# Two-layer graph network: the packed adjacency turned by DMA as 16-bit numbers in place of TensorE transposes

## What is computed

```
deg = clip(adj.sum(1), 1); dis = deg ** -0.5
diffusion = (dis[:,None] * adj * dis[None,:]) @ x - x
sim  = cosine similarity of all pairs of rows of x
attn = softmax(beta * sim * adj, axis=1)
x1 = layernorm(x + diffusion + sigmoid(alpha) * (attn @ x - x))
out = layernorm(x1 + relu(adj @ (x1 @ weights)))
```

## Time and profile before

| | us |
|---|---|
| median of 3 runs | 677.5 (676.59 to 679.42) |
| the profiled execution's own time | 677.66 |
| span of the profiled execution, first to last instruction | 675.8 |
| PE busy | 652.8 |
| DVE busy | 534.2 |
| ACT busy | 414.1 |
| POOL busy | 244.9 |

### The profile page before, as it was taken

How to read it: one execution, slowest core, us unless ns; L and a number is a source line. 1 busy time by engine, 2 the same in 40 slices (tenths; PEclk the granted TensorE clock), 3 DMA queues, 4 the chain that set the end, 5 groups by cost and what they waited for, 6 DMA issues and landing times.

```text
span 675.8 us, 16373 instructions
## 1 busy us (share of the span) xinstructions
PE 652.8 (97%) x5143; PEld 470.1 (70%) x5143; DVE 534.2 (79%) x1598; ACT 414.1 (61%) x775; POOL 244.9 (36%) x229
## 2 busy tenths in 40 slices
PE   6779999999999999999999999899999999999996
PEld 6447777777777777777777777788888864444455
DVE  4879999999999999999999999877777762334442
ACT  5989899898998999988999988511111110000000
POOL 2899446446455465454465467300000000000000
PEclk8999999999999999999999999999999999999999
DMA  6589999999999999999999994300000000000000
GB/s 252 185 220 249 242 261 244 253 255 243 260 263 242 254 253 249 250 266 232 262 260 249 249 248 94 67 1 1 0 0 0 0 0 1 17 16 16 16 31 32
DMA packets 154539, 105.33 MB, mean 156 GB/s; under 512 B 135696, under 2 KB 136208, under 8 KB 154512
## 3 DMA queue, kind: packets, MB, share of 16 engines
q1 hardware_dynamic: 154080, 104.94, 61.0%
q10 hardware_dynamic: 432, 0.07, 0.1%
HBM read 69.34 MB, written 2.10 MB: 106 GB/s over the span
## 4 chain that ended last, share of the span: by engine, by line
PE 85%; DVE 4%; DMA 3%; POOL 3%; ACT 2%; SPq 1%; issue 1%; DVEq 0%; ACTq 0%; POOLq 0%
PE ps_s L974 21%; PE ps_s L1135 17%; PE ps_e L1107 14%; PE ps_e L1006 8%; PE ps_e L985 7%; PE ps_acc L1006 7%; PE ps_e L1009 4%; PE ps_acc L1009 3%; DMA eTx<-e_parts 2%; DVE e_parts L710 1%; DMA col<-in_L_gnn_beta 1%; PE ps_e L1022 1%; DVE scores L689 1%; PE ps_at L958 1%; SPq L242 1%; POOL x_parts L339 1%
## 5 line engine op out<-in xcount | busy, mean ns | idle before, releaser
L974 PE MATMUL ps_s<-xn_parts,xn_signed 128*128 128x512 f16 x756 | 203.7, 379 | 5.1 <-DVE cmax L689 5.1
L689 DVE CUSTOM_DVE_ANT_1 scores<-ps_s,adj_bytes 128x512 f32<-128x512 f32 x252 | 171.6, 683 | 17.1 <-PE ps_s L974 10.3
L500 ACT ACTIVATE scores<-scores,col 128x1024 f32<-128x1024 f32 x128 | 157.4, 1232 | 4.3 <-DVE col L700 4.1
L324 POOL TENSOR_SCALAR e_parts<-scores 128x1024 f16<-128x1024 f32 x64 | 84.0, 1313 | 158.2 <-ACT scores L500 93.0
L446 ACT ACTIVATE adj_bytes<-land 128x1024 uint8<-128x1024 f32 x128 | 133.5, 1047 | 1.8 <-POOL packed L316 1.8
L974 PEld LDWEIGHTS ps_s<-xn_parts,xn_signed 128*128 128x128 f16 x756 | 69.5, 98 | 41.3 <-DVE cmax L689 5.1
L1107 PE MATMUL ps_e<-y_parts,stage 128*128 128x256 f16 x896 | 98.0, 273 | 0.0
L710 DVE SCALAR_TENSOR_TENSOR e_parts<-scores,e_parts 128x1024 f16<-128x1024 f32 x64 | 97.0, 1516 | 0.9 <-POOL e_parts L324 0.9
L507 ACT ACTIVATE eT_parts<-ps_e 128x512 f16<-128x512 f32 x128 | 75.8, 592 | 32.0 <-PE ps_e L985 31.2
L1107 PEld LDWEIGHTS ps_e<-y_parts,stage 128*128 128x128 fp8e4 x896 | 87.7, 98 | 10.1
L704 DVE SCALAR_TENSOR_TENSOR eT_parts<-ps_e,eT_parts 128x512 f16<-128x512 f32 x128 | 87.5, 684 | 1.5 <-ACT eT_parts L507 1.5
(11 more groups left out here) (131 smaller groups left out, 1015.0 us busy)
## 6 DMA issues: line engine op xcount, KB each, us to landing
land<-in_adj SPq DMA_DIRECT2D x128, 512.0 KB, 4.7
x_keep<-in_x SPq DMA_DIRECT2D x4, 512.0 KB, 8.4
out<-u SPq DMA_DIRECT2D x7, 256.0 KB, 2.0
eTx<-e_parts SPq DMA_TRANSPOSE x64, 4.6
out<-u SPq DMA_DIRECT2D x2, 128.0 KB, 1.7
eT_parts<-in_L_gnn_weights ACTq DMA_DIRECT2D x1, 64.0 KB, 8.6
scores<-in_L_gnn_weights SPq DMA_DIRECT2D x1, 64.0 KB, 2.8
col<-in_L_gnn_alpha ACTq DMA_DIRECT2D x1, 0.5 KB, 5.6
```

The lines of the kernel that those rows point to most:

```text
L324: nc.gpsimd.tensor_scalar(e_parts[:, n, 0, :], scores[:, q, (n + 2) * CH:(n + 3) * CH], E_SCALE, 1.0, ALU.mult, ALU.mult).wait_op(sign_don ...
L500: nc.scalar.activation(piece, piece, ACT.Exp, bias=neg_max[q], scale=abs_beta, accum_out=csum[:, q, i:i + 1]).then_inc(exp_done, 1)
L689: nc.vector.tensor_tensor_reduce(scores[:, q, o:o + BANK].rearrange("p (k q) -> p k q", k=K), score_bank(h, r == 0 if start else False).re ...
L974: ins = nc.tensor.matmul(score_bank(h, start), xn_signed[:, q, part, :], xn_parts[:, other, o:o + BANK], start=(part == 0 and other == 0), ...
```

## The change

K becomes 2: a node's number is b*256 + 2*p + k, with 16 blocks b of 256 nodes. Two neighbouring bytes, a 16-bit number, now belong to one position of two blocks.

- A byte of the packed row holds two row blocks: the even row of a pair is cast to 128, 64, 32, 16, the odd one to 8, 4, 2, 1. `pack` of the even row is three additions as before; `pack` of the odd row adds its four pieces to the same word, so it is four.
- `turn_adj` leaves PE. Once in two rows the SP queue issues one DMA transpose of 128 partitions x 512 16-bit numbers (128 KB), 16 in all, directly into packT. In the loop it stands behind pieces 2 and 3 of a row and ahead of turn n = 0 of an odd row; the last one is behind the last turn.
- `store_adj` and its semaphore are gone, so DVE has one copy less a row. packT is half as large.
- `stage_block` reads the word of the pair and shifts left or, for the top bit, right. The number of instructions and their shapes stay.
- Order inside each bank of 512 columns: SLOT = (0, 2, 1, 3) names which block of x stands in which quarter. Mask, transposes, `attend` and `sign_block` use it; `sign_block` and `pack` on POOL are written out for four rows at a time.
- Moving and stationary fp8 reads have a step of 2 bytes and the mask's byte read too, in place of 4. x is loaded and the output stored in runs of 1 KB in place of 2 KB.

```diff
-K = 4
-BYTE_ONE = 64
+K = 2
+BYTE_TOP = (128, 8)
+BYTE_F8_BITS = 0x40404040
...
-        packT = sb("packT", [P, R, CH // K], U32)
+        packT = sb("packT", [P, R // 2 * W], U32)
...
-            sp.dma_start(x_b[:, 0:2, :], x_v[:, 0:2, :]).then_inc(x_loaded[0], 16)
-            for q in range(1, C):
-                sp.dma_start(x_b[:, 2 * q:2 * q + 2, :], x_v[:, 2 * q:2 * q + 2, :]).then_inc(x_loaded[q], 16)
+            for q in range(C):
+                sp.dma_start(x_b[:, 4 * q:4 * q + 4, :], x_v[:, 4 * q:4 * q + 4, :]).then_inc(x_loaded[q], 16)
...
+            def turn_adj(m, q):
+
+                sp.wait_ge(packed_done, 2 * m + 2)
+                sp.dma_start_transpose(packT[:, bass.ds(m * W, W)].bitcast(U16).rearrange("p (a i) -> p a i", i=P),
+                                       packed_half[q]).wait_op(x_loaded[0], 16, "sem-ge").then_inc(adj_turned, 16)
+
...
+            turn_adj(0, 0)
+            with sp.Fori(1, Q) as b:
+                for k in range(G):
+                    r, q = b * G + (k - 3), (k + 1) % 2
                     for i in range(C):
...
                         if i == 1:
                             turn_ex(r, q, 1)
+                    if k == 1:
+                        turn_adj(b * 2 + (-1), 1)
+                    if k == 3:
+                        turn_adj(b * 2, 0)
                     turn_ex(r + 1, 1 - q, 0)
             for r in (R - 3, R - 2, R - 1):
                 turn_ex(r, r % 2, 1)
                 if r < R - 1:
                     turn_ex(r + 1, (r + 1) % 2, 0)
+            turn_adj(R // 2 - 1, 1)
...
-            def pack(r, q, first=False):
+            def pack(r, q, m, s, first=False):
 
 
                 pool.wait_ge(cast_done, r * C + C)
...
+                if q == 0:
+                    if not first:
+                        pool.wait_ge(adj_turned, m * 16 - 16)
+                    nc.gpsimd.tensor_tensor(packed[:, s, :], words[q][:, 0, :], words[q][:, 1, :],
+                                            ALU.add).then_inc(pack_step, 1)
...
+                else:
+                    pool.wait_ge(packed_done, r)
+                    for i in range(C - 1):
+                        nc.gpsimd.tensor_tensor(packed[:, s, :], packed[:, s, :], words[q][:, i, :],
+                                                ALU.add).then_inc(pack_step, 1)
+                        pool.wait_ge(pack_step, m * 5 + (3 + i))
+                nc.gpsimd.tensor_tensor(packed[:, s, :], packed[:, s, :], words[q][:, 3, :],
                                         ALU.add).then_inc(packed_done, 1)
...
-            def store_adj(r):
-
-                dve.wait_ge(adj_turned, r + 1)
-                nc.vector.tensor_copy(packT[:, r, :], ps_at[:, 0:CH // K].bitcast(U32)).then_inc(adj_stored, 1)
-
...
+                    up = 6 - ((3 if n % 2 else 7) - i)
+                    nc.vector.tensor_scalar(stages[to][:, bass.ds(n, 1), i * W:(i + 1) * W],
+                                            packT[:, bass.ds(r * P + (-P if n % 2 else 0), W)].unsqueeze(1), abs(up),
+                                            BYTE_F8_BITS, ALU.logical_shift_left if up >= 0 else ALU.logical_shift_right,
                                             ALU.bitwise_and).then_inc(staged, 1)
...
-                    if h == 6:
-                        store_adj(r)
...
-                    if h == 1:
-                        turn_adj(r, q, start)
```

More of the change, by code:

```diff
@@ L202, in two_layer_gnn @@
         x_v = x.rearrange("(b p k) d -> p b (k d)", p=P, k=K)
-        out_v = out.rearrange("(b p k) d -> b p (k d)", p=P, k=K)
-        adj_v = adj.rearrange("(b p k) j -> b k p j", p=P, k=K)
+        out_v = out.rearrange("(g b p k) d -> g p b (k d)", b=G // K, p=P, k=K)
+        adj_v = adj.rearrange("(g b p k) j -> g b k p j", b=G // K, p=P, k=K)
         u_b = u[:, :, :].rearrange("p (b k) d -> p b (k d)", k=K)
@@ L218, in two_layer_gnn @@
         words = [adj_bytes[:, q, :].bitcast(U32).rearrange("p (i w) -> p i w", i=C) for q in range(2)]
-        packed_f = [packed[:, q, :].bitcast(F32) for q in range(2)]
+        packed_half = [packed[:, m, :].bitcast(U16) for m in range(2)]
         stages = [land[:, :, :].bitcast(U32), stage[:, :, :]]
@@ L247, in _ @@
                 land_piece(0, 0, i)
-            for k in range(1, K):
+            for k in range(1, G):
                 for i in range(C):
@@ L251, in _ @@
                     land_piece(0, k, i)
-                    if k == K - 1 and i == 1:
+                    if k == G - 1 and i == 1:
                         turn_ex(0, 0, 1)
-                if k == K - 2:
+                if k == G - 2:
                     turn_ex(0, 0, 0)
-                if k == K - 1:
+                if k == G - 1:
                     turn_ex(1, 1, 0)
-            with sp.Fori(1, B) as b:
-                for k in range(K):
-                    r, q = b * K + (k - 3), (k + 1) % 2
+            turn_adj(0, 0)
+            with sp.Fori(1, Q) as b:
+                for k in range(G):
+                    r, q = b * G + (k - 3), (k + 1) % 2
                     for i in range(C):
-                        sp.wait_ge(cast_done, b * (K * C) + ((k - 1) * C + i + 1))
+                        sp.wait_ge(cast_done, b * (G * C) + ((k - 1) * C + i + 1))
                         land_piece(b, k, i)
@@ L273, in _ @@
             sp.dma_start(wts, weights).then_inc(w_loaded, 16)
[L274 to L280, removed]
+            with sp.Fori(0, Q - 1) as g:
+                sp.wait_ge(out_done, g * G + G)
+                sp.dma_start(out_v[g], u_b[:, bass.ds(g * 2, 2), :]).then_inc(out_stored, 16)
+            for b in range(2):
+                sp.wait_ge(out_done, R - 2 + 2 * b)
+                sp.dma_start(out_v[Q - 1, :, b, :], u_b[:, B - 2 + b, :]).then_inc(out_stored, 16)
+            sp.wait_ge(out_stored, 16 * (Q + 1))
         @block.gpsimd
@@ L348, in _ @@
             for i in range(C):
-                nc.gpsimd.memset(deg_unit[:, i:i + 1], float(1 << i) / BYTE_ONE).then_inc(deg_step, 1)
+                for q in range(2):
+                    nc.gpsimd.memset(deg_unit[:, i, q:q + 1], 1.0 / (BYTE_TOP[q] >> i)).then_inc(deg_step, 1)
             unit_rows(1)
@@ L359, in _ @@
             x_split(1)
-            pack(0, 0, first=True)
+            pack(0, 0, 0, 0, first=True)
             ex_high(0, 0, 0, first=True)
             ex_high(0, 0, 1, first=True)
-            sign_block(2, 0)
+            sign_block(2, 0, 2)
             x_split(2)
@@ L366, in _ @@
             ex_high(1, 1, 0)
-            pack(1, 1, first=True)
+            pack(1, 1, 0, 0)
             ex_high(1, 1, 1)
-            sign_block(3, 1)
+            sign_block(3, 1, 3)
             pool.wait_ge(sigma_done, 1)
@@ L403, in _ @@
             ex_high(R - 2, 0, 1)
-            pack(R - 1, 1)
+            pack(R - 1, 1, R // 2 - 1, 1)
             pool.wait_ge(dis_done, 1)
@@ L590, in _ @@
             keep_z(0, G)
-            for j in range(1, B - 1):
+            for j in range(1, Q - 1):
                 keep_z(j, G)
                 roots(j - 1, G)
[L594 to L598, removed]
+            keep_z(Q - 1, 2)
+            roots(Q - 2, G)
+            keep_z(Q, 2)
+            roots(Q - 1, 2)
+            roots(Q, 2)
         @block.vector
@@ L916, in _ @@
                 stage_block(G + n, n)
-            for j in range(1, B):
+            for j in range(1, Q):
                 relu_add(j - 1, (j - 1) * G, G)
-                if j < B - 1:
+                if j < Q - 1:
                     dve.wait_ge(z_done, j)
@@ L948, in turn_rows @@
                 ins.then_inc(xnt_turned, 1)
[L950 to L960, removed]
             def cosines(r, q, h, start=False):
@@ L1004, in attend @@
                     else:
-                        hi, lo = (eTx[:, q, b // 2 - 2, a * TC + t % TC, :] for a in range(2))
+                        hi, lo = (eTx[:, q, b // 2 - 2, a * TC + slot, :] for a in range(2))
                     nc.tensor.matmul(attn_ps[q][:, 0:2 * D], hi, x_parts[:, t, :],
```

107 lines of the change are left out of this document (52 added, 55 removed).

## The result

| | before | changed |
|---|---|---|
| median | 677.24 us (4 runs) | 665.62 us (4 runs, 664.87 to 666.40) |
| ratio to before | | 0.9828, 95% interval 0.9814 to 0.9841 |
| profiled execution, time and span | 677.66, 675.8 | 666.40, 664.5 |

The account below looks back on a forecast made before the run. PE was taken to bound the row phase without slack, with the SP queue 0.6 us a pair behind and taking over after the change. 677.7 + 6.0 - 0.7 - 0.5 = 682.5 us, range 667 to 693.

Parts of the forecast that it names:

- PE's two transposes: Row phase on PE: removing them frees 0.22 us a row, 0.44 in a pair, 7.0 us over 32 rows.
- DVE's copy and POOL's additional addition: Copy hidden in the row phase, 0.7 us saved behind the last rows; addition hidden, 0 with bounds -0.8 and +0.8.
- the 0.7 + 0.5 of the sum: Savings of 0.7 us for two DVE copies behind the last rows and 0.5 for PE's slots in rows 0, 1, 30, 31.
- The 16 DMA turns: SP queue in the row phase: 1.03 us more in a pair, lengthening pairs by 0.43, +6.0 us in all.
- a turn isn't put out before what stands ahead of it on the queue has nearly drained: SP queue: turns end some 4.6 to 5.0 us after the landings were issued, read as waiting for the drain.
- four halves of 6.1 us are the least: SP queue's least time for a pair of rows, taken as 24.4 us beside 25.0 measured.
- a slack of 0.6 us: SP queue's spare time in a pair of rows, seen as idle DMA engines from 252.50 to 253.00 us.
- Its upper bound: New turns on the SP queue: 1.32 us to put out whatever the size, no overlap, 26.35 a pair, +19 us.
- 0.33 if it goes with size: Time to put out a new turn on the SP queue, scaled from 1.32 us for 2048 numbers.
- The reads with a step of 2: Second layer's fp8 matmuls: 0 taken, bounds -4.6 and 0 us, as jumps between row blocks could explain the times too.
- x in runs of 1 KB: Loading x at the very start: 0 taken, bounds -0.5 and +1.5 us.
- Rival B with the reads: Turn fits into idle half microsecond before odd row's T0 turn, PE stays bound: 670 us, 665.7 if reads count; chance 0.33.

Follow-up runs that it names:

- pe_back: Changed kernel with two dummy 128 x 128 f32 transposes a row put back on PE, without DVE's copy: 671.37 us.
- before_flat4: Kernel before, second layer reading each 512 columns out of one row block at a step of 4 bytes, no jumps: 677.49 us.
- after_step4: Changed kernel, second layer reading the staged bytes with a step of 4 bytes instead of 2: 669.51 us.
- before_step2: Kernel before, second layer reading with a step of 2 bytes instead of 4: 672.47 us.
- split2: Changed kernel with every long turn of the numerators (128 x 2048) issued as two of 128 x 1024: 666.55 us.
- before_step8: Kernel before, second layer reading with a step of 8 bytes instead of 4: 793.68 us.

## Why the prediction was wrong, by its steps

- **PE's two transposes**: right. 0.22 us a row from the earlier trace rows, 0.23 measured in pe_back; that start-to-start reading and not the 0.39 of busy time. PE was named as having no gap, and from row 6 on it has none after either.
- **DVE's copy and POOL's additional addition**: right, hidden in the row phase. Row 30 to the sum phase gained 1.2 us, which equals the 0.7 + 0.5 of the sum, but no run puts the copies or the transposes back into the last two rows, so the two sizes are not shown apart, and the 0.5 was meant for rows 0 and 1 as well.
- **The 16 DMA turns**: the step that failed. The queue's least pair was to grow from 24.4 to 25.43 us and to take the row phase over, +6.0 us in 28 rows with PE's gain already lost in it. Rows 6 to 30 took 6.5 us less (24.46 a pair), and a row takes 12.23 us with the turns and without. This is 12.5 of the 16.9 us between 682.5 and 665.6. Two of its parts were wrong. First, "a turn isn't put out before what stands ahead of it on the queue has nearly drained" was read from long turns only, and of its two rows just the T1 turns bear it out: the T0 turn at 251.96 ended as late because its data came late. The short one is held 1.19 us, and the run split in two shows a hold only when both landings and a first half lie ahead. Second, "four halves of 6.1 us are the least" took the pace of a queue that is fed by the other engines for its own limit: in the changed kernel halves of 5.76 us occur, and a pair with one short turn more still takes 24.5. Part of this nobody forecast: landings are faster in the changed kernel (4.4 in place of 4.7 us), and two long turns a pair are held for 0.5 us less each (4.2 in place of 4.7). Whether the turn would be as free with the old landings wasn't tried; the 3.3 us of room in the earlier trace rows says that it would. What I called a slack of 0.6 us, the idle half microsecond of the earlier trace rows, was larger by the time during which the queue waited for the T0 turn's data: 3.3 us behind the landings in the earlier trace rows, into which two short turns of 1.2 fit.
- **Its upper bound** (a fixed 1.32 us to put a turn out) was right about that part, with 1.19 measured; "0.33 if it goes with size", which I took, was wrong. It had no effect because the time lay in a wait. The rate of a turn's data, 203 GB/s, didn't matter either: the 0.63 us that I worked out from it shows in no pair of rows, 24.46 us with the new turn and 24.46 without.
- **The reads with a step of 2**: -5.0 us where I took 0 and had -4.6 as bound. The rows had f16 matmuls at 0.217 and fp8 ones at 0.226; I let the jumps explain the difference. before_flat4 shows that they cost nothing. One alternative cause was enough to make me take nothing for a term whose size was read rightly.
- **x in runs of 1 KB**: not shown either way. In the profiled execution the second squares of x start at 10.13 in place of 9.14 and row 0 at 34.42 in place of 33.77, but in after_step4, which loads x the same way, at 8.23 and 32.48, and in before_step2 at 8.46 and 32.63. Executions of one start-up differ by more than these two kernels do.
- **Rival B with the reads** is what happened, by its own two mechanisms: 665.7 against 665.6 measured. That it agrees to 0.1 us is luck: in the profiled pair its pieces are off by -0.3 in the rows, -0.4 in the reads and +1.4 in the start, and it knew nothing of the faster landings. I gave B a third, and its end with the reads lay outside my range.

## What to carry to other kernels

A queue that is busy all the time isn't thereby full: before adding to it, look for the instruction that waits for data from an engine, and see whether the new one, at its own measured time to be put out, ends before that data is ready. Here the T0 turn waited until 3.3 us behind the landings, and a turn of 1.19 us fitted in. A hold measured on one size needn't carry over to a smaller one: 4.32 us for the long turn behind landings and 1.19 for the short one. On the moving side of a matmul, the byte step of an fp8 read is worth a look of its own (0.216, 0.226 and 0.452 us for 512 columns at 2, 4 and 8 bytes), and it can be tried alone in a one-line change.

## What was not expected of the hardware

- Putting out a DMA turn on the SP queue takes nearly the same for 128 x 512 and 128 x 2048 16-bit numbers: 1.19 us, 0.24 us behind two landings (changed kernel), and 1.32 us, 3.3 us behind them (kernel before).
- A long turn behind two landings holds the queue for some 4.2 us in the changed kernel (4.7 before), the first half of it alone for 1.25 (split2).
- Landings of the same 512 KB pieces take 4.7 us before and 4.4 in the changed kernel, for a reason that wasn't isolated.
- fp8 matmuls of 512 columns take 0.216, 0.226 and 0.452 us at a step of 2, 4 and 8 bytes (before_step2, before, before_step8).
